# Weighing expert outputs in feature rows on Pool instead of transposing all of them, in a two-layer vision tower with mixtures of experts

## The reference

```
# layer 0 experts: x is (tokens, 64), normalised by layer norm
hid_e = relu(n @ W1[e].T + b1[e])            # 256 hidden features
y_e   = hid_e @ W2[e].T + b2[e]              # 64 features
w     = top-2 of softmax(n @ Wg.T + bg), made to sum to 1 (0 for the other 6)
h     = h + sum_e w[token, e] * y_e
# layer 1: x = x + attention(...) @ wo.T;  then RMS norm, and experts
hid_e = silu(n @ w1[e].T) * (n @ w3[e].T)    # 170 hidden features
h     = h + x + sum_e w[token, e] * (hid_e @ w2[e].T)
```

## Time and profile before

| | us |
|---|---|
| median of 3 runs (1220.97 to 1228.97) | 1227.97 |
| the profiled execution | 1219.27 |
| its span, first to last instruction | 1217.5 |
| busy in it: TensorE | 1081.6 |
| Vector | 879.7 |
| Scalar | 608.3 |
| Pool | 458.1 |

### The profile page before, as it was taken

One profiled execution on the slowest core, in us unless ns is written; L12 is line 12 of the kernel. 1 busy time (PEld: TensorE's weight loads), 2 busy tenths in 40 slices (PEclk: granted clock), 3 DMA queues, 4 the chain that ended last, 5 costly groups with the idle time before them and its releaser, 6 DMA issues. The chain is left out here.

```text
span 1217.5 us, 23980 instructions
## 1 busy us (share of the span) xinstructions
PE 1081.6 (89%) x8420; PEld 811.2 (67%) x8420; DVE 879.7 (72%) x2104; ACT 608.3 (50%) x1269; POOL 458.1 (38%) x613
## 2 busy tenths in 40 slices
PE   6795877959999999997588969988799999999996
PEld 2464776746777777775474547768687777777774
DVE  1696656966777777775678769973677888877874
ACT  2254774636556655653324437770554454554552
POOL 2373001211434434434326478730033433333334
PEclk8797999969999999999698989995799999999998
DMA  8100000000000000000000000000000000000000
GB/s 246 83 1 1 2 1 2 1 1 1 2 1 1 1 1 2 1 1 1 1 1 1 1 1 3 2 3 1 1 7 6 7 6 7 6 12 6 7 7 12
DMA packets 3455, 13.57 MB, mean 11 GB/s; under 512 B 400, under 2 KB 2192, under 8 KB 2960
## 3 DMA queue, kind: packets, MB, share of 16 engines
q1 hardware_dynamic: 3056, 8.00, 2.3%
q0 software_dynamic: 288, 4.11, 0.9%
HBM read 9.97 MB, written 2.13 MB: 10 GB/s over the span
## 5 line engine op out<-in xcount | busy, mean ns | idle before, releaser
L1306 PE MATMUL moe_psU<-moe_nT_parts,moe_w_hi 128*128 128x320 f32 x988 | 325.4, 340 | 1.7 <-ACT moe_nT_parts L1048 0.9
L1306 PE MATMUL moe_psU<-moe_nT_parts,moe_w_lo 128*128 128x320 f32 x988 | 297.4, 311 | 0.0
L1306 PEld LDWEIGHTS moe_psU<-moe_nT_parts,moe_w_hi 128*128 128x128 f32 x988 | 188.5, 191 | 56.6 <-issue 50.1
L1306 PEld LDWEIGHTS moe_psU<-moe_nT_parts,moe_w_lo 128*128 128x128 f32 x988 | 189.1, 191 | 0.0
L1210 DVE TENSOR_TENSOR moe_hid<-moe_psU,moe_silu 128x320 f32<-128x320 f32 x286 | 139.4, 491 | 62.3 <-ACT moe_silu L1074 52.6
L1001 POOL TENSOR_TENSOR moe_sum<-moe_scaled 128x256 f32<-128x256 f32 x130 | 99.1, 763 | 171.1 <-DVE moe_scaled L1200 170.5
L1074 ACT ACTIVATE moe_silu<-moe_psU 128x320 f32<-128x320 f32 x286 | 125.5, 439 | 56.5 <-PE moe_psU L1306 39.2
L1079 ACT ACTIVATE moe_hid<-moe_psU,middle 128x320 f32<-128x320 f32 x260 | 129.5, 528 | 34.1 <-PE moe_psU L1306 31.8
L126 POOL TENSOR_TENSOR moe_stats<-moe_stats,minus_half 128x5 f32<-128x5 f32 x26 | 31.5, 1213 | 274.6 <-DVE moe_stats L1123 274.6
L1216 DVE TENSOR_SCALAR moe_hid<-moe_psU,middle 128x320 f32<-128x320 f32 x156 | 85.7, 550 | 67.5 <-PE moe_psU L1306 66.7
L1317 PE MATMUL moe_psY<-moe_hid,middle 128*64 128x320 f32 x832 | 124.8, 442 | 0.7 <-ACT moe_hid L1079 0.7
(11 more groups left out here) (301 smaller groups left out, 1982.5 us busy)
## 6 DMA issues: line engine op xcount, KB each, us to landing
images<-in_x SPq DMA_DIRECT2D x8, 576.0 KB, 11.0
late<-in_late POOLq DMA_DIRECT2D x1, 2456.5 KB, 12.5
out_tokens<-h SPq DMA_DIRECT2D x13, 160.0 KB, 1.8
middle<-in_middle POOLq DMA_DIRECT2D x1, 1554.0 KB, 7.4
early<-in_early SPq DMA_DIRECT2D x1, 1042.5 KB, 18.8
early<-in_early SPq DMA_DIRECT2D x1, 80.0 KB, 2.0
```

What stands on the lines that cost most here:

```text
L1306: last = pe.matmul(psum[:, 0:HALF], w[:, col:col + SPLIT], moving, start=(part == 0), stop=(part == 1))
```

## The change

1. In all tiles but the last of each layer, the expert outputs are weighed where `y` has them, in feature rows. The routing weights of a tile are turned by one transpose (to [5 x 8 rows, 128 images]), copied by Scalar (`keep_weights`), written to a DRAM scratch, and read back by two DMAs, each of which repeats them over 64 partitions (`wide`, 128 x 4 x 640, 1311 KB in all, one buffer). Pool multiplies `y` by `wide` in four products and adds them in three sums of 128x640 to `total` (`weigh_wide`); five transposes turn `total` to token-major in the body after the next (`back`); Vector adds the two halves while it reads PSUM (`read_back`), and Pool adds that to the residual (`add_back`).
2. The last tile keeps the old way (`token_major`, `weigh`, `add_last`).
3. In layer 1 the logits move from place (0,0) to (0,2), with the slots of the routing behind them. The loops of Pool and SyncE are written out.
4. `output1`: the weight is the stationary matrix, two tiles side by side on the two halves of the array; Scalar copies the result, five transposes turn a pair of tiles, Vector adds to x and Pool adds x to h.

```diff
         if layer == 0:
             LOGITS, DOWN = (0, 2), 4
-            OUTS = [(0, 7), (1, 2), (1, 7), (2, 2), (2, 6)]
+            BACK, READ = [(1, 4)], [(1, 6)]
             TURN = [(3, 2)]
-            WEIGH = [(0, 7), (1, 3), (1, 7), (2, 3), (2, 7)]
-            HI, KEEP, EXP = (1, 5), [(3, 2)], (3, 0)
+            KEEP_W, HI, KEEP, EXP = (0, 6), (1, 5), [(3, 2)], (3, 0)
         else:
-            LOGITS, DOWN = (0, 0), 1
-            OUTS = [(0, 3), (1, 0), (1, 3), (2, 0), (2, 2)]
+            LOGITS, DOWN = (0, 2), 1
+            BACK, READ = [(1, 1), (2, 1)], [(1, 2), (2, 2)]
             TURN = [(3, 1), (3, 3)]
-            WEIGH = OUTS
-            HI, KEEP, EXP = (1, 3), [(3, 1), (3, 3)], (0, 3)
+            KEEP_W, HI, KEEP, EXP = (0, 4), (1, 3), [(3, 1), (3, 3)], (0, 5)
-            SLOTS = {(0, 1): "aaaannn", (1, 1): "neeeeee", (2, 1): "neeeeee", (3, 1): "eeeeeee"}
+            SLOTS = {(0, 3): "aaaannn", (1, 1): "neeeeee", (2, 1): "neeeeee", (3, 1): "eeeeeee"}
...
+                def add_back(n):
+                    pool.wait_ge(back_read, PARTS * (n + 1))
+                    tile = resid[:, n * T:(n + 1) * T, :]
+                    pool.tensor_tensor(tile, tile, both[:, :, :], ALU.add).then_inc(added, 1)
+                    pool.wait_ge(added, n + 1)
+
+                def weigh_wide(n):
+                    mine, into = y[n % 2], total[n % 2]
+                    pool.wait_ge(wide_in, 32 * (n + 1))
+                    pool.wait_ge(y_out, PAIRS * (n + 1))
+                    for p in range(PAIRS):
+                        chain.link(pool.tensor_tensor(mine[:, p, :], mine[:, p, :], wide[:, p, :], ALU.mult))
+                        if p == 1:
+                            need(pool, back_mm, PARTS * (n - 1))
+                            chain.link(pool.tensor_tensor(into[:, :], mine[:, 0, :], mine[:, 1, :], ALU.add))
+                        elif p == 2:
+                            chain.link(pool.tensor_tensor(into[:, :], into[:, :], mine[:, 2, :], ALU.add))
+                    pool.tensor_tensor(into[:, :], into[:, :], mine[:, PAIRS - 1, :], ALU.add).then_inc(total_set, 1)
...
+                for g in range(NT):
+                    if g < NT - 1:
+                        deviation(g + 1)
+                    if g >= 2:
+                        add_back(g - 2)
+                    if g >= 1:
+                        weigh_wide(g - 1)
...
+                def widen(n):
+                    sp.wait_ge(wT_set, n + 1)
+                    need(sp, wide_in, 32 * n)
+                    sp.dma_start(scratch.rearrange("e t b -> t e b"), weightsT[:, :]).then_inc(wT_out, 16)
+                    sp.wait_ge(wT_out, 16 * (n + 1))
+                    need(sp, total_set, n)
+                    for side in range(2):
+                        rows = scratch.rearrange("(p s) t b -> s p (t b)", s=2)[side:side + 1]
+                        sp.dma_start(wide[D * side:D * side + D, :, :], rows.to_broadcast([D, PAIRS, TOK])).then_inc(wide_in, 16)
...
+                def keep_weights(n):
+                    act.wait_ge(L_mm, n + 2)
+                    act.wait_ge(L_read, n + 2)
+                    need(act, wT_out, 16 * n)
+                    act.copy(weightsT[:, :], weights_ps).then_inc(wT_set, 1)
...
+                def read_back(n, part):
+                    t0, t1 = TURNS[part]
+                    dve.wait_ge(back_mm, PARTS * n + (part + 1))
+                    if part == 0:
+                        need(dve, added, n)
+                    halves = psM[:, 0:(t1 - t0) * 128].rearrange("b (t s d) -> b t d s", s=2, d=D)
+                    dve.tensor_reduce(both[:, t0:t1, :], halves, axis=AX.X, op=ALU.add).then_inc(back_read, 1)
...
                 def logits(g, slot):
                     pe.wait_ge(nTr_set, (g + 1) * len(TURNS))
-                    need(pe, scaled_set, (g - 1) * T)
+                    if g >= 1:
+                        pe.wait_ge(routed, g)
+                        pe.transpose(weights_ps, weights[:, (g - 1) * T:g * T, :].rearrange("b t e -> b (t e)"), ident)
...
+                def back(n, part):
+                    t0, t1 = TURNS[part]
+                    if part == 0:
+                        pe.wait_ge(total_set, n + 1)
+                        pe.wait_ge(L_read, min(n + 3, NT))
+                        pe.wait_ge(wT_set, min(n + 2, NT - 1))
+                    else:
+                        pe.wait_ge(back_read, PARTS * n + part)
+                    for t in range(t0, t1):
+                        last = pe.transpose(psM[:, (t - t0) * 128:(t - t0 + 1) * 128], total[n % 2][:, t * B:(t + 1) * B], ident)
+                    last.then_inc(back_mm, 1)
...
-                        if before:
-                            for t in range(T):
-                                if OUTS[t] == (p, k):
-                                    if t == 0:
-                                        pe.wait_ge(L_read, g + 1)
-                                    token_major(g - 1, 1 - slot, t)
+                        if g >= 2 and (p, k) in BACK:
+                            back(g - 2, BACK.index((p, k)))
```

```diff
-def output1(nc, late, h, x, yT):
+def output1(nc, late, early, h, x, yT):
...
+                def project(k):
+                    g, n = PAIRS[k]
+                    need(pe, sides_set, k - 1)
+                    for begin, cols in pieces():
+                        for s in range(n):
+                            at = (g + s) * TOK + begin
+                            last = pe.matmul(psA[k % 2][D * s:D * s + D, begin:begin + cols], late[:, c["wo1"]],
+                                             yT[:, at:at + cols], start=True, stop=True)
+                    last.then_inc(A_mm, 1)
```

129 lines of the change are left out of this document (77 added, 52 removed).

## The result

The changed kernel takes 1297.99 us (median of 4 runs, 1282.59 to 1303.57), the kernel before 1228.47 (1220.97 to 1232.62, 4 runs): a ratio of 1.053 with an interval of 1.042 to 1.065. One of the four runs (1303.57) was in the slow state, and the ratio is taken from the other three, whose median is 1294.28. It is slower by 66 to 70 us; the forecast was 1264, in a range of 1213 to 1295. The profiled execution is the fastest of the four (1282.59 us, span 1280.8).

The account below looks back on a forecast made before the run. TensorE was taken to bound both expert stages; transposes -18.4 and -15.5, stalls +39.6 and +28.8, layer ends +2 and +3, attention output -3 made +36.5 us on 1219.3, so 1255.8; with the median 8.7 above, 1264, range 1213 to 1295.

Parts of the forecast that it names:

- What bounds: Expert stages: TensorE bounds; its added work or stalls count once per tile, Vector and Pool nothing until TensorE waits for them.
- Part 1: TensorE in the bodies: fewer transposes gain 1.53 us per tile in the first layer, 1.29 in the second; -18.4 and -15.5 us.
- Part 2: Pool's chain per tile: seven 128x640 operations of 1.64 us each, pitch 1.72, chain 12.1 us, some 12.3 with its wait.
- Part 3: Routing's end: Pool's chain holds Vector's two-SBUF-input operations, stalling TensorE 3.3 and 2.4 us a tile; +39.6 and +28.8 us.
- rival 3: First layer: two Vector operations slip through each Pool gap, no stall there; 1225 us, chance 0.13 with mixtures.
- rival 1: Vector is held, but never where TensorE waits, since the chain comes at another time; -32, 1196 us, chance 0.15.
- Part 4: Moved logits, earlier `routed`, Vector's and Scalar's changed work, stores and fetches: waits at nothing, taken as 0 us.
- Part 5: Ends of the layers: the last totals and the old way for the last tile come later; +2 and +3 us.
- Part 6: New attention output: 25 us against 28, near the slow end of the clock; -3 us (0 to -12).
- 2: Rival: the transfer into the one `wide` buffer plus Pool's chain bounds the period, from 9.1 us on; 1295 us, chance 0.12.

Follow-up runs that it names:

- split_back: `one_op_early` with the first layer's five transposes of the totals one by one at five places instead of one batch; 22.32 us per first-layer body, one run.
- one_op: The changed kernel with only one 128x640 product of Pool's chain left, the other products and the sums left out; 1196.56 us, ratio 0.978.
- one_op_early: `one_op` with the second layer's logits moved back to (0,0) and its routing steps to (0,1); 1183.15 us, one run.
- memset: The changed kernel with six of Pool's seven chain operations replaced by fills of 128x1600 and the last by one of 128x640; 1215.48 us, one run.
- late_chain: The changed kernel with Pool's chain also waiting until the next tile's routing is done; 1275.7 us, one run.
- output_only: The kernel before with nothing but the new attention output; 1218.12 us, ratio 0.992.
- quarters_early: The changed kernel with each of Pool's chain operations cut in four of 160 columns and the second layer's logits back at (0,0); 1275.82 us, ratio 1.038.
- halves: The changed kernel with each of Pool's seven chain operations cut in two of 320 columns; 1236.70 us, ratio 1.007.
- mixed: The kernel before with the new attention output and, in the first layer alone, the change with Pool's chain halved; 1214.12 us, ratio 0.992.

## Why the prediction was right, and where it was off

The direction and the mechanism held. By the 1294.28 us the time came out 30 us above the forecast, just inside the range; by the median of all four it is 34, and 3 above the range. That it is so near owes something to luck, since errors of 4 to 27 us in the terms stand partly against each other. Of the 30, 27 are in the profiled execution (1282.6 for 1255.8); the rest is that the median lies 12 us above that execution, where 8.7 had been added.

**What bounds** held: TensorE's stalls count one for one, until the stalls pull its clock down, which then counts too.

**Part 1** was too high in the first layer: 0.84 us per body, not 1.53 (about 8 us over the layer). The sum took the batches' full price off, but `split_back` shows that a batch is partly free where it stands between up steps that would wait for their banks. In `one_op` 16 steps between up passes of a first-layer body take 0.20 to 0.26 us in place of 0.147, in the kernel before 13; over the body what they take beyond 0.147 is 1.6 us against 1.2, so some 0.4 of the missing 0.7 us are there. The rest is not taken apart; that the 0.44 us of the earlier trace rows hold such a slow step beside the batch (from the pass at 302.98, in the cut of those rows, to 303.21) may be part of it. The second layer has 26.19 - 24.90 = 1.29, as forecast, but by luck: with the logits at (0,0) the gain is 26.19 - 24.58 = 1.61 (`one_op_early`), and the move took 0.32 of it back.

**Part 2** held: 1.55 us an operation (1.55 to 1.64 given, 1.64 taken), pitch 1.63 for 1.72, the chain 11.3 us for 12.3.

**Part 3**, the step that decides, held in kind. The wait does grow with Pool's operation; the halved chain, the single product and the fills show it from three sides. The Trainium skill (SBUF — State Buffer, "SBUF: two separate sides") has the port pair blocked for the whole instruction, and these rows agree up to 1.57 us. The same section has a Vector operation with two SBUF inputs meet only an operation of GpSimd's that reads SBUF, and one in a two-port mode any of them. `memset` agrees with the first (0.17 to 0.20 us under fills); that L1212 with one input is held by fills fits the second, but no row shows its mode. Pool's power doesn't fit the section: 1.17 us, two SBUF inputs, and nothing held. So the forecast's rule, a Vector operation with two SBUF inputs ends no sooner than Pool's, is too wide there and too narrow for L1212, which it left out (it is L1164 in the kernel before). The size was a little high: 2.59 us per body for 3.3, 2.09 for 2.4. In the first layer one of the four named operations slipped through in every body, as 0.20 us at 391.07, where Pool's gap was 0.08 us, so rival 3's doubt was right for one operation of four. The chain came later than worked out: its body starts near 366.77 - 1.54 - 0.6 = 364.6 by TensorE's timeline, and the chain at 386.21, 21.6 us in, not 15.3. Scalar's copy of the weights, at 375.28, was already 10.7 us in, not 6.5, since stall and half clock lie at the body's start; the write took 2.0 us (375.56 to 377.59, 1.8 forecast), the rest is the transfer, 8.6 for 7. The routing's end had moved too: L1214 at 389.69 is 25.1 us in, not 18.9, so the chain still covered it. That is luck: rival 1's own condition, a start after 19 us, was met, and its outcome did not come. With `late_chain`'s phase the stall is there too.

**Part 4** had a real mistake: "Moving the second layer's logits from (0,0) to (0,2): the routing starts 1.2 us later with 7 us of slack". That weighed the routing against its own due time, not against its cover. Its first seven steps lost the down product beside them, and that costs 1.03 us of idle time, 1.35 us per body in all, about 15 us over the layer. The other zeros (`routed`, read-back, copies, fetches) held: `one_op` has them all and stands still nowhere else.

**What no part had** is the clock. The earlier trace rows show 1.00 in both stages, and I kept that while adding stalls. It fell after them, at a price of 1.56 and 0.78 us per body, (37.5 + 17.1) / 2 = 27 us for the stretches of both layers. This is the largest single term of the miss.

**Part 5**: 40.5 - 11 x 3.46 = 2.4 us and 34.4 - 11 x 2.71 = 4.6, for +2 and +3. These still hold the twelfth body of each layer, which the forecast counted elsewhere; with twelve taken off they are -1.0 and 1.9, so the first agrees by luck.

**Part 6** was too small: -11.5 us, not -3, near the far end of its range (-12). The step that failed is the choice of the clock: I carried the 0.50 of the earlier trace rows over, and the clock was 1.00 in this stage (0.89 in `output_only`). The passes themselves were priced right, at 13.3 us for the 12 given at 2.4 GHz.

**The sum by terms**, from the forecast's +36.5 to the measured +63.3 of the span: +8 (Part 1), -8 and -4 (the stalls of Part 3 over eleven or twelve tiles), +12 (the wait in Part 4), +27 (clock), +2 (ends), -8.5 (Part 6) make +65. The terms are rounded and not cut alike, over eleven bodies or twelve, so a remainder of 2 means nothing. **Rivals**: 1 did not come, and `late_chain` has the stall at a second phase too; 2 is out by the 7.6 us landing, under its 9.1 (the estimate by the Trainium skill, SBUF — State Buffer, "Door 1: The DMA port swizzle", was 7.8, and this trace agrees; `quarters_early` shows that the ring that binds first is another one); 3 is out by three held operations of the four named, where it had two slip through each gap.

## What to carry to other kernels

Before giving Pool long products or sums of two SBUF tiles, find Vector's small operations that stand ahead of an eviction TensorE waits for, those with two SBUF inputs and, as L1212 shows, some with one, and cut Pool's operations so that a hold fits into the slack there; but a cut that lengthens the chain must still fit its ring of dependences. When a step is moved, ask what stood beside it and hid it, not only when its result is due. And where a change puts waits into a stage that ran at full clock, price the clock too: here it cost 27 us beside 62 us of waits in eleven bodies of each layer.

## What was not expected of the hardware

- Half clock after short waits: stretches of 3.4 us (some 6.8) behind waits of 1.5 to 2.9 us, though TensorE had been busy all the rest of a 25 us body. Behind the single waits of 1.03 us in `one_op` there was none in eleven bodies; behind the nine of 1.95 to 1.97 us in `halves` there were two stretches. Two kernels with the same 2.09 us wait had 17.1 and 54.4 us of it; what makes the difference stays open.
- Pool's fills of 1.43 us did not hold Vector's operations with two SBUF inputs at all (0.17 to 0.20 us each), but held one with a single input (L1212, 1.0 us by the median, 0.16 alone). Its products and sums of 1.55 us held both kinds to their own end. Its power of 1.17 us with two SBUF inputs held neither.
- The stages ahead of the first layer differ by up to 13 us from run to run of like code: it starts at 256.1 us in `mixed` and at 269.1 in `memset`. Runs with a single time carry that uncertainty, which is why the bodies and not the times are compared for them.
